# Handing one of seven pair sums of the exponentials from GpSimd to VectorE in a cross-attention kernel

## The reference, cut to what matters

```python
def _L0_xattn_ref(x, context, context_mask, Wq, Wk, Wv, Wo, bo, g1, b1, g2, b2):
    xn = _layer_norm(x, g1, b1)
    cn = _layer_norm(context, g2, b2)
    q = (xn @ Wq.T).reshape(B, Tx, HEADS, HEAD_DIM)
    k = (cn @ Wk.T).reshape(B, Tc, HEADS, HEAD_DIM)
    v = (cn @ Wv.T).reshape(B, Tc, HEADS, HEAD_DIM)
    scores = jnp.einsum('bqhs,bkhs->bhqk', q, k) / np.sqrt(HEAD_DIM)
    scores = jnp.where(context_mask[:, None, None, :], scores, -jnp.inf)
    attn = jax.nn.softmax(scores, axis=-1)
    out = jnp.einsum('bhqk,bkhs->bqhs', attn, v).reshape(B, Tx, C)
    return out @ Wo.T + bo
...
x = x + _L0_xattn_ref(_layernorm(x), ctx_1024, mask, ...)
x = x + _L0_ffn_ref(_layernorm(x), L0_ffn_weight, L0_ffn_bias)   # blocks of 32 quantised to fp6
```

## Time and profile before

| | before |
|---|---|
| median of 3 runs | 4435.17 us (4431.02 to 4442.58) |
| the profiled execution | 4433.29 us, span 4431.5 us |
| PE busy | 4264.6 us, 96% of the span |
| DVE busy | 3400.1 us, 77% |
| POOL busy | 2938.9 us, 66% |
| ACT busy | 2850.1 us, 64% |

### The profile page before, as it was taken

How to read it: one execution, slowest core, us unless ns; L and a number is a source line. 1 busy time by engine, 2 the same in 40 slices (tenths; PEclk the granted TensorE clock), 3 DMA queues, 4 the chain that set the end, 5 groups by cost and what they waited for, 6 DMA issues and landing times.

```text
span 4431.5 us, 89201 instructions
## 1 busy us (share of the span) xinstructions
PE 4264.6 (96%) x36496; PEld 1486.4 (34%) x36496; DVE 3400.1 (77%) x3967; ACT 2850.1 (64%) x5184; POOL 2938.9 (66%) x1830
## 2 busy tenths in 40 slices
PE   4999999999999999999999999999999999999998
PEld 2322343223432234322342223422234222342223
DVE  5788667886688865888658886688866888668875
ACT  3387744877448864478655886558755587546884
POOL 2299652996539954499534995359953599426993
PEclk9999999999999999999999999999999999999999
DMA  5256642657326573356733566335664366543654
GB/s 182 71 121 125 158 143 62 125 119 187 115 62 128 115 200 102 71 117 124 191 101 77 115 125 184 106 79 119 124 174 110 78 122 127 167 112 78 126 124 107
DMA packets 193708, 539.67 MB, mean 122 GB/s; under 512 B 28737, under 2 KB 102785, under 8 KB 152082
## 3 DMA queue, kind: packets, MB, share of 16 engines
q0 software_dynamic: 43776, 318.79, 36.0%
q1 hardware_dynamic: 149522, 215.17, 15.6%
HBM read 118.32 MB, written 21.01 MB: 31 GB/s over the span
## 4 chain that ended last, share of the span: by engine, by line
PE 66%; DVE 20%; ACT 4%; DMA 3%; POOL 3%; issue 3%; SPq 0%; DVEq 0%; ACTq 0%; POOLq 0%
PE banks L1114 17%; PE banks L1126 16%; PE banks L1022 16%; PE banks L1082 11%; DVE max_parts L663 11%; PE banks L1157 4%; PE banks L991 2%; ACT region L892 2%; DMA sums<-wkT_wvT_wqT 1%; PE banks L1016 1%; POOL wkT_wvT_wqT L453 1%; DVE amax L611 1%; ACT values L972 1%; DVE x_stats L573 1%; DVE region L801 1%
## 5 line engine op out<-in xcount | busy, mean ns | idle before, releaser
L663 DVE TENSOR_REDUCE max_parts<-banks 128x2 f32<-128x1024 f32 x2048 | 2397.1, 1217 | 409.4 <-PE banks L1082 393.4
L892 ACT ACTIVATE region<-banks 128x512 f32<-128x512 f32 x4096 | 2190.5, 607 | 452.5 <-PE banks L1114 401.6
L453 POOL TENSOR_TENSOR wkT_wvT_wqT<-region 128x1024 f32<-128x1024 f32 x528 | 1313.0, 2632 | 464.6 <-PE banks L1126 273.0
L1114 PE MATMUL banks<-queries_stacked,keys_stacked 98*32 98x512 f16 x16384 | 1264.2, 382 | 12.5 <-ACT values L876 6.2
L1126 PE MATMUL banks<-region,values 128*32 128x512 f32 x8192 | 1076.0, 599 | 17.7 <-ACT region L892 14.2
L1082 PE MATMUL banks<-keys_stacked,queries_stacked 33*128 33x512 f16 x4096 | 724.0, 385 | 31.8 <-DVE max_parts L663 28.3
L1114 PEld LDWEIGHTS banks<-queries_stacked,keys_stacked 98*32 98x32 f16 x16384 | 401.3, 95 | 1000.3 <-ACT region L892 599.4
L1022 PE MATMUL banks<-region,wkT_wvT_wqT 128*128 128x512 f16 x2304 | 556.7, 380 | 13.2 <-DMA wkT_wvT_wqT<-weights_split 10.6
L1082 PEld LDWEIGHTS banks<-keys_stacked,queries_stacked 33*128 33x128 f16 x4096 | 184.2, 93 | 649.1 <-issue 354.1
L453 POOL TENSOR_TENSOR sums<-region 128x1024 f32<-128x1024 f32 x144 | 373.0, 2729 | 9.1 <-ACT region L892 9.1
L433 POOL TENSOR_TENSOR region<-row_sums_inverse,region 128x512 f16<-128x512 f32 x80 | 93.0, 1163 | 429.5 <-ACT region L855 428.9
(11 more groups left out here) (99 smaller groups left out, 3232.4 us busy)
## 6 DMA issues: line engine op xcount, KB each, us to landing
wdT<-wkT_wvT_wqT POOLq DMA_DIRECT2D x96, 1024.0 KB, 12.0
wkT_wvT_wqT<-wkT_wvT_wqT POOLq DMA_DIRECT2D x80, 1024.0 KB, 7.3
sums<-wkT_wvT_wqT POOLq DMA_DIRECT2D x72, 1024.0 KB, 7.4
wkT_wvT_wqT<-sums POOLq DMA_DIRECT2D x40, 1024.0 KB, 7.4
region<-in_x SPq DMA_DIRECT2D x24, 1024.0 KB, 8.6
wkT_wvT_wqT<-weights_split SPq DMA_DIRECT2D x8, 3072.0 KB, 20.6
keys_stacked<-region SPq DMA_DIRECT2D x384, 64.0 KB, 2.0
keys_stacked<-sums SPq DMA_DIRECT2D x384, 64.0 KB, 2.0
```

Of the source, the lines that this page charges most:

```text
L453: e.tensor_tensor(SUMS[dst][:, half], PR[i][:, half], PR[i + 1][:, half], ALU.add).then_inc(s_pr, 1)
L663: e.tensor_reduce(mpart[:, buf, :, a, t, c], MXB[parity], AX.X, ALU.max).then_inc(s_mxd, 1)
L892: e.activation(PR[u % 4][:, j * HALF:j * HALF + HALF], score_bank(m % NU, kt, j)[0], ACT.Exp, scale=SCALE).then_inc(s_ex, 1)
L1114: mm = e.matmul(dst[HD * t:HD * t + HD, :], KA[0:STR, ds(ka + (j * C + (u + 1) * P + HD * t), HD)], QA[0:STR, ds(qa[j], HALF)], start=True ...
```

## The change

VectorE adds pair 2 (tiles 4 and 5) in units 0 to 6. Half 0 stands behind its two reductions of step 4, half 1 behind those of step 5. GpSimd no longer makes pair 2 and, before pair 3, waits until all six halves of pairs 0 to 2 are counted.

```diff
@@ GpSimd, a unit but the last
-                        e.wait_ge(s_pv, n * KT + 4 + (3 if g + q == 0 else 4))
-                        pair(2, two)
                         if g + q > 0:
                             e.wait_ge(s_ac2, late * 16)
+
+                        e.wait_ge(s_pr, n * 14 + 2 + 6)
                         pair(3, three)
                         merge(1, 2, two)
@@ VectorE, in unit()
+                    def third_pair(h):
+                        two = buffers(n)[2]
+                        half = ds(2 * HALF * h, 2 * HALF)
+                        if h == 0:
+                            e.wait_ge(s_pr, m * 14 + 2 + 4)
+                            e.wait_ge(s_pv, m * KT + 4 + (3 if n == 0 else 4))
+                        e.wait_ge(s_ex, m * (KT * J) + 5 * J + 2 * h + 4)
+                        e.tensor_tensor(SUMS[two][:, half], PR[0][:, half], PR[1][:, half], ALU.add).then_inc(s_pr, 1)
+
                     end = last and q == 1
                     if not end:
                         for t in range(QT):
                             max_row(idx + 8 + 2 * t, 1 - q, QT + t)
+                            if t < 2:
+                                third_pair(t)
                         maxima(1 - q, n + 1, idx + 16)
```

## The result

The changed kernel takes 4451.75 us (median of 8 runs, 4448.5 to 4456.09); the kernel before took 4436.77 us in the same comparison (8 runs, 4431.02 to 4442.58). The ratio is 1.0036, with a 95% interval of 1.0026 to 1.0045: slower by 12 to 20 us. I had forecast slower, with 4467 us and a range of 4444 to 4489; the way was right, the size was twice too large.

What follows compares the result with a forecast made beforehand. TensorE, paced in places by VectorE, was taken as the bound, with GpSimd's load mostly hidden. Unit 0's 2.2, units 1 to 5's 5 x 0.2 and unit 6's 0.8 us, x 8, gave 32 us: 4467 us, range 4444 to 4489.

Steps and rivals of the forecast that it cites:

- Bound and covers: TensorE and GpSimd nearly full; VectorE has one gap per half except in unit 0; GpSimd's load hidden except ending unit 6.
- Unit 0, forecast 2.2 us: In unit 0, VectorE's additions fall where 0 and 0.17 us are idle: +1.19 and +1.02, taken as 2.2 us.
- My lower bound, 1.9: Least growth forecast for unit 0, in us, if the 0.33 us of looser place before step 9 is given back.
- Units 1 to 5, forecast 0.2 us each: Gaps of about 1.05 us nearly take each half; remaining lateness reaches TensorE in step 7: 0.2 us a unit, 1.0 a batch.
- step 5's reductions are 0.14 late, step 6's 0.30: In units 1 to 5, how late in us each addition makes VectorE's following reductions; TensorE's step 7 then starts 0.27 later.
- GpSimd's delay, forecast 1.1 us: GpSimd's pair 3 waits for VectorE's half 1, starting 1.1 us later; covered in units 1 to 5, costing 0.8 in unit 6.
- the one that I had said would grow, 0.70 to 1.5: ScalarE's wait for GpSimd before tile 0 of unit 7, said to grow from 0.70 to 1.5 us.
- Sum: Whole kernel: 2.2 + 5 x 0.2 + 0.8 = 4.0 us a batch, x 8 = 32 us, giving 4467 us.
- rival 2: Gaps take the halves, GpSimd's shift vanishes, unit 0 gets back half its price: 11 us, 4446 us; chance 0.12.
- The port: VectorE's half 0 may wait for GpSimd's L497, both reading SBUF: up to 0.6 us in some 6 of 40 places.
- The covered case: Units 1 to 6 absorb halves and most of GpSimd's shift; unit 0 recovers half its price: 4446 us, chance 0.12.
- The relief of GpSimd: Removing 5 of GpSimd's 43 us ends unit 6 earlier and removes waits before and in unit 7: -17 us, 4418; chance 0.07.

Runs made afterwards that it cites:

- Unit 0 alone: Against the kernel before, VectorE adds pair 2 in unit 0 only, GpSimd keeping it in units 1 to 6: 4451.51 us, ratio 1.0033.
- the multiplications: VectorE adds pair 2 in units 1 to 5 only; there GpSimd also runs two 128x1024 fp32 multiplications before pair 3: 4570.88 us, ratio 1.0302.
- A version of it that pays: Against the kernel before, pair 2 stays on GpSimd and VectorE adds pairs 5 and 6 of unit 6: 4421.93 us, ratio 0.9961.

## Why the prediction was right, and where its sizes were off

- **Bound and covers.** That VectorE has almost no room in unit 0, one gap for each half in units 1 to 6, and that GpSimd's load is hidden but for the end of unit 6, all held. The cost fell where the argument put it: unit 0 and unit 6.
- **Unit 0, forecast 2.2 us, measured 1.8.** The mechanism was right. The term was mis-sized because I took the rows' durations and idle times as if they lay end to end. An addition costs 1.13 us from start to start and not 1.19; my own rows gave about 1.14, since 2 x 1.217 - 2.36 is 0.07 and not the 0.03 that I took off. And the real slack of the two steps was 5.01 - 2 x 2.27 = 0.47 us and not 0.17. It is made of the 0.17, of 0.12 between steps 4 and 5, where I wrote that nothing is idle, and of two overlaps of 0.09. 2 x 1.13 - 0.47 = 1.79. My lower bound, 1.9, was not low enough either.
- **Units 1 to 5, forecast 0.2 us each, measured 0.** The same error: a gap that reads 1.06 us is 3.41 - 2.27 = 1.14 from start to start, and 1.13 fits. The step "step 5's reductions are 0.14 late, step 6's 0.30" did not happen. What was said to follow from lateness did hold once there was lateness: 0.66 late, 0.54 passed on.
- **GpSimd's delay, forecast 1.1 us.** In unit 6 step 5's reductions start at 1033.52 and pair 3 at 1037.14, 3.62 later; before it was 2.72. So 0.9: I had step 5's two reductions at 2.41 us, where they take 2.27 from start to start. Of the 0.9, 0.64 arrived at ScalarE, forecast 0.8. It arrived at the first of ScalarE's two waits, 0.22 to 0.86; the one that I had said would grow, 0.70 to 1.5, stayed at 0.70. In the other units nothing waits for it, as forecast.
- **Sum.** 8 x (1.79 + 0.64) = 19 us, against a measured 12 to 20; the terms of units 1 to 5 (8 us), 0.4 in unit 0 (3 us) and 0.2 in unit 6 (1 us) are what lay above it. Unit 0 alone, 14 us, is nearly all of the measured 15; unit 6's 5 us are in the profiles and not in the timed runs.
- **The range held partly by luck.** 4451.75 us is 1 us under my own forecast's range of 4453 to 4485 and nearer to the 4446 of rival 2 than to my 4467. The wider range of 4444 to 4489 holds it only because it was stretched for that rival.
- **The port.** One of the 40 additions behind L497 met it, by 0.17 us, and took 1.27 us. The other 39 started 0.08 to 0.98 us behind its end, so that it is so few is chance of some tenths of a microsecond; what it costs where GpSimd is busy, the multiplications showed.
- **Rivals.** The covered case was right for five units and wrong for unit 0, which gave nothing back: that the time came out near its 4446 isn't its mechanism. The relief of GpSimd paid nothing, as pair 3 waited for VectorE. A version of it that pays exists where VectorE is idle, but only together with the DMA that comes next.

## What to carry to other kernels

To see whether one more instruction fits into a gap, take the distance between the starts of the two neighbours and subtract the start-to-start distance of the same work on a busy stretch; the profile's duration plus idle time counts the overlap of neighbouring rows as occupied. Balance between engines by total busy time says little: the same addition was free beside row sums, cost 0.9 us where VectorE paced TensorE, and took 2.8 us longer on average where it met a multiplication on GpSimd. A row that joins several instructions can hide small gaps between them; ask for the group's idle time too. When work changes hands, look at what the former owner now waits for, and behind a removed wait for the DMA that is next in line.

## What I had not expected of the hardware

TensorE's granted clock falls to half (0.5, that is 1.2 GHz instead of 2.4) for 3.4 us at a time: four times in the profile of the kernel before, six in that of the changed one, for the most part in other batches. In the changed kernel one such stretch lies in unit 0 of the last batch (the unit, and the stretch in it):

```profile
4033.60:4076.88 43.28, 41.20 (x447) 11.67 (x443) 36.00 (x32) 34.76 (x66) 31.19 (x17) 0.96 0.37 74
...
4035.60:4039.00 3.40, 3.33 (x20) 0.67 (x20) 0.00 (x0) 1.93 (x5) 2.23 (x1) 0.51 0.02 5
```

That unit took 43.28 us where the one of the third batch took 41.88: 1.4 us for one stretch. TensorE had been idle twice shortly before the clock fell:

```profile
4033.02 0.83 PE L1126 MATMUL banks<-queries_stacked,keys_stacked 98*32 98x512 f16 x12 [0.78 <-ACT values L888]
4034.20 0.40 PE L1126 MATMUL banks<-queries_stacked,keys_stacked 98*32 98x512 f16 x4 [0.35 <-ACT region L904]
```

The first batch has the same two gaps and the same fall behind them. The other six batches have the same two gaps at the same place, and the clock stays at 1.00 there, so these gaps alone don't decide it. The four falls outside unit 0 came behind 1.8 to 2.3 us of idle time of TensorE. Where TensorE had to wait more, the falls were more: 23 in the run with the multiplications. Single units have to be compared with those that have none. The median doesn't do that by itself: in unit 0, three of the eight batches before and two of the eight after have one.
